# A four-layer graph network: the last layer run as one stage, block by block, with no barrier between its two sums

## The reference

```python
def _gcn_conv(x, W, b, src, dst, n):
    h = x @ W
    s = concat([src, loop]); d = concat([dst, loop])
    deg = segment_sum(ones_like(d), d, n)
    dinv = rsqrt(deg)
    msg = (dinv[s] * dinv[d])[:, None] * h[s]
    return segment_sum(msg, d, n) + b
h = relu(_gcn_conv(x, W1, b1, src, dst, n))
z = _gcn_conv(h, W2, b2, src, dst, n)
x = _layernorm(x + z)
```

## Time and profile before

| | us |
|---|---|
| median of three runs | 4654.02 |
| the profiled execution's own time | 4652.1 |
| its span, first to last instruction | 4650.3 |
| busy: PE, DVE, POOL, ACT | 2810.4, 3001.2, 2727.2, 934.8 |
| last layer: first matmul of the first sum to the end of the span | 342.9 |

### The profile page before, as it was taken

How to read it: one execution, slowest core, us unless ns; L and a number is a source line. 1 busy time by engine, 2 the same in 40 slices (tenths; PEclk the granted TensorE clock), 3 DMA queues, 4 the chain that set the end, 5 groups by cost and what they waited for, 6 DMA issues and landing times. The chain is left out here.

```text
span 4650.3 us, 56109 instructions
## 1 busy us (share of the span) xinstructions
PE 2810.4 (60%) x18074; PEld 2599.7 (56%) x18075; DVE 3001.2 (65%) x6284; ACT 934.8 (20%) x781; POOL 2727.2 (59%) x2656
## 2 busy tenths in 40 slices
PE   1356656656614555556566456666666667994955
PEld 0356656656613555555556356655665657983744
DVE  6355655655676666676665477777777778996144
ACT  0121221211201222222221121221221123441000
POOL 0577777777705777777773277777777723551000
PEclk9566656656656677776668767777777779996977
DMA  1444444444404455445443356556655625540532
GB/s 20 109 98 110 102 99 109 100 102 109 98 21 103 134 135 136 136 132 136 135 133 90 84 138 154 147 146 153 153 144 149 153 56 123 115 106 1 171 95 92
DMA packets 169458, 526.18 MB, mean 113 GB/s; under 512 B 60851, under 2 KB 87800, under 8 KB 156470
## 3 DMA queue, kind: packets, MB, share of 16 engines
q1 hardware_dynamic: 74032, 299.78, 26.1%
q0 software_dynamic: 95264, 224.28, 18.6%
HBM read 456.40 MB, written 67.48 MB: 113 GB/s over the span
## 5 line engine op out<-in xcount | busy, mean ns | idle before, releaser
L544 POOL DMA_INDIRECT e0G<-table,e0src x858 | 851.9, 993 | 439.1 <-issue 405.1
L544 POOL DMA_INDIRECT e21G<-table,e21src x858 | 856.1, 998 | 408.1 <-issue 257.6
L1364 POOL DMA_INDIRECT t1G<-table,t1idx x806 | 789.7, 980 | 375.5 <-issue 242.0
L1437 PE MATMUL t1psW<-t1CO,t1G 128*128 128x192 f32 x1612 | 435.9, 434 | 303.9 <-issue 285.6
L1437 PEld LDWEIGHTS t1psW<-t1CO,t1G 128*128 128x128 f32 x1612 | 370.4, 258 | 312.2 <-issue 292.2
L568 PE MATMUL e21psQ<-Q,e21OT 121*128 x1716 | 412.5, 410 | 129.6 <-DVE e21G L682 54.3
L568 PEld LDWEIGHTS e21psQ<-Q,e21OT 121*128 121x128 f32 x1716 | 399.8, 326 | 141.4 <-issue 81.6
L561 PE MATMUL e0psQ<-Q,e0OT 121*128 x1716 | 398.7, 371 | 94.3 <-ACT e0OT L599 58.2
L561 PEld LDWEIGHTS e0psQ<-Q,e0OT 121*128 121x128 f32 x1716 | 396.6, 325 | 99.8 <-issue 99.8
L2103 POOL TENSOR_TENSOR e22Z<-e22Z,e22C 121x847 f32<-121x847 f32 (+1 forms) x104 | 200.1, 1955 | 259.0 <-ACT e22Z L2095 259.0
L584 PE MATMUL e21psA<-e21G,e21O 128*121 128x145 f32 x1716 | 272.4, 330 | 106.1 <-DVE e21G L733 106.1
(11 more groups left out here) (428 smaller groups left out, 5250.8 us busy)
## 6 DMA issues: line engine op xcount, KB each, us to landing
e0dstb<-in_dst_p SPq DMA_DIRECT2D x27, 1996.5 KB
e21dstb<-in_dst_p SPq DMA_DIRECT2D x27, 1996.5 KB
e22C<-counts SPq DMA_DIRECT2D x26, 1487.0 KB
Q<-in_type_p SPq DMA_DIRECT2D x62, 416.0 KB
counts<-X SPq DMA_DIRECT2D x13, 1487.0 KB
planes<-SKIP SPq DMA_DIRECT2D x26, 743.5 KB
counts<-RES SPq DMA_DIRECT2D x13, 1487.0 KB
e31C<-planes SPq DMA_DIRECT2D x26, 743.5 KB
```

The lines of the kernel that those rows point to most:

```text
L544: nc.gpsimd.indirect_dma_start(out=G[:, u, t, 0:width], out_offset=None, in_=table, in_offset=bass.IndirectOffsetOnAxis(ap=src[:, u, t:t + ...
L1364: nc.gpsimd.indirect_dma_start(out=G[:, q % 2, t, :], out_offset=None, in_=table, in_offset=bass.IndirectOffsetOnAxis(ap=idx[:, q * GT + t ...
L1437: mmi = nc.tensor.matmul(psW[:, k % 2, 0:WIN * NBAS], G[:, q % 2, t, :], CO[:, k % 2, i].rearrange("p b w -> p (b w)"), start=(i == 0), st ...
```

## The change

The first projection stays. The other five stages become one function, `last_layer`, with one block of engine programs.

TensorE, in the first sum: after the 26 matmuls of block b it waits until its own last matmul is done, and only then gives the buffer back (`buffer_free`), turns the finished rows of block b-1 (`turn`) and multiplies those of block b-2 with W2 (`make`). In the second sum it waits in the same way after every block. VectorE, in the first sum: `take` adds the three parts and then into `SKIP` (so `RES` is not cleared and `SKIP` not added later), one operation scales and adds the bias, and `row` scales the product with W2 and splits four blocks at a time into a second set of parts, `HP2`. Relu is ScalarE's copy out of PSUM. In the second sum VectorE finishes each block as it comes and normalizes two blocks at a time; SyncE stores two blocks at a time. W2 and both biases are loaded ahead of the first counts. The counts of the second sum go through the same ring and are loaded as the first sum frees buffers. The only meeting point left is `parts_ready`: the second sum starts when all seven groups of `HP2` are written.

The diff, without the allocation of buffers:

```diff
@@ -171,10 +171,8 @@
 
         with ExitStack() as ctx:
             g["HP"] = ctx.enter_context(nc.sbuf_tensor("HP", [BN, NB, 3, D], BF16))
-            for c in (1, 2):
-                project(g, f"p3{c}", [(f"L3_gnn_W{c}", None)], tab[128], "gcn", source=X if c == 1 else RES)
-                dense_sum(g, f"e3{c}")
-                gcn_finish(g, f"f3{c}", f"L3_gnn_b{c}", out if c == 2 else None)
+            project(g, "p31", [("L3_gnn_W1", None)], tab[128], "gcn")
+            last_layer(g, out)
@@ -2155,6 +2153,228 @@
             dve.drain()
 
 
+def last_layer(g, out):
+    nc, a, X, RES, SKIP, HP, planes, eye, cnt1 = (g[k] for k in ("nc", "a", "X", "RES", "SKIP", "HP", "planes", "eye", "cnt1"))
+    RING = NB // 2
+    GRP = 4
+    NGRP = -(-NB // GRP)
+    STORES = (16 * 8, 16 * 6)
...
+        S = {n: sem(n) for n in ("consts", "waited", "buffer_free", "summed", "taken", "row_ready", "row_turned", "row_copied", "row_made",
+                                 "row_taken", "parts_ready", "summed2", "taken2", "var_ready", "rooted", "block_ready")}
...
+        @block.sync
+        def _(sp):
+            n = n_planes(sp)
+            def load(b, k, done):
+                sp.wait_ge(S["buffer_free"], done + 1)
+                sp.sem_inc(S["waited"], 1)
+                sp.dma_start(C[:, b % RING].rearrange("p h d -> p (h d)"),
+                             planes[bass.ds(k * NB + b, 1)].rearrange("a l n -> (a l) n")).then_inc(counts_in[b % RING], 16)
+            def store(k, i):
+                sp.wait_ge(S["block_ready"], k * (NB // 2) + (i + 1))
+                sp.sem_inc(S["waited"], 1)
+                if 2 * i + 2 < NB:
+                    sp.dma_start(out[2 * i * BN:(2 * i + 2) * BN].rearrange("(b p) f -> p b f", p=BN), z[:, i % 2]).then_inc(stored[i % 2], 16)
+                else:
+                    sp.dma_start(out[2 * i * BN:(2 * i + 1) * BN], z[:, i % 2, 0]).then_inc(stored[i % 2], 16)
+                    sp.dma_start(out[(2 * i + 1) * BN:N], z[0:N - (2 * i + 1) * BN, i % 2, 1]).then_inc(stored[i % 2], 16)
+            sp.dma_start(w2[:], a["L3_gnn_W2"]).then_inc(S["consts"], 16)
+            for i in range(2):
+                sp.dma_start(bias[:, i, :], a[f"L3_gnn_b{i + 1}"].partition_broadcast(BN)).then_inc(S["consts"], 16)
+            with sp.Fori(0, n) as k:
+                for b in range(NB):
+                    load(b, k, k * NB + b)
+            with sp.Fori(0, n) as k:
+                for b in range(NB):
+                    load(b, k, n * NB + k * NB + b)
+                    if b % 2 == 1 and b >= RING:
+                        store(k, b // 2 - RING // 2)
+                for i in range((NB - 1) // 2 - RING // 2 + 1, NB // 2):
+                    store(k, i)
+            for u in range(2):
+                sp.wait_ge(stored[u], n * STORES[u] + 16)
+                sp.sem_inc(S["waited"], 1)
+        @block.tensor
+        def _(pe):
+            n = n_planes(pe)
+            def sums(b, parts, made):
+                for h in range(NB):
+                    mmi = nc.tensor.matmul(ps[0:BN, b % 2, 0:3 * D], C[:, b % RING, h, :],
+                                           parts[:, h].rearrange("p k f -> p (k f)"), start=(h == 0), stop=(h == NB - 1))
+                mmi.then_inc(made, 1)
+            def turn(b, k):
+                pe.wait_ge(S["row_ready"], k * NB + (b + 1))
+                pe.wait_ge(S["row_copied"], k * NB + (b + 1))
+                nc.tensor.transpose(psT[:, b % 2, 0:BN], y[:, b % 2, :], eye[0:BN, 0:BN]).then_inc(S["row_turned"], 1)
+            def make(b, k):
+                pe.wait_ge(S["row_copied"], k * NB + (b + 3))
+                pe.wait_ge(S["row_taken"], k * NB + (b + 1))
+                nc.tensor.matmul(psY[0:BN, b % 2, 0:D], hT[:, b % 2, :], w2[:], start=True, stop=True).then_inc(S["row_made"], 1)
+            pe.sem_inc(S["buffer_free"], RING)
+            pe.sem_inc(S["row_made"], 2)
+            pe.wait_ge(S["consts"], 48)
+            with pe.Fori(0, n) as k:
+                for b in range(NB + 2):
+                    if b < NB:
+                        pe.wait_ge(counts_in[b % RING], k * 32 + (b // RING * 16 + 16))
+                        pe.wait_ge(S["taken"], k * NB + (b + 1))
+                        pe.sem_inc(S["waited"], 1)
+                        sums(b, HP, S["summed"])
+                        pe.wait_ge(S["summed"], k * NB + (b + 1))
+                        pe.sem_inc(S["buffer_free"], 1)
+                    if 1 <= b <= NB:
+                        turn(b - 1, k)
+                    if b >= 2:
+                        make(b - 2, k)
+            with pe.Fori(0, n) as k:
+                for b in range(NB):
+                    pe.wait_ge(counts_in[b % RING], n * 32 + k * 32 + (b // RING * 16 + 16))
+                    pe.wait_ge(S["taken2"], k * NB + (b + 1))
+                    if b == 0:
+                        pe.wait_ge(S["parts_ready"], n * NGRP)
+                    pe.sem_inc(S["waited"], 1)
+                    sums(b, HP2, S["summed2"])
+                    pe.wait_ge(S["summed2"], k * NB + (b + 1))
+                    pe.sem_inc(S["buffer_free"], 1)
+        @block.scalar
+        def _(act):
+            n = n_planes(act)
+            act.sem_inc(S["row_copied"], 2)
+            with act.Fori(0, n) as k:
+                for b in range(NB):
+                    act.wait_ge(S["row_turned"], k * NB + (b + 1))
+                    act.wait_ge(S["row_made"], k * NB + (b + 1))
+                    nc.scalar.activation(hT[:, b % 2, :], psT[:, b % 2, 0:BN], ACT.Relu).then_inc(S["row_copied"], 1)
+            with act.Fori(0, n) as k:
+                for i in range(NB // 2):
+                    act.wait_ge(S["var_ready"], k * (NB // 2) + (i + 1))
+                    nc.scalar.activation(var[:, i % 2, :], var[:, i % 2, :], ACT.Sqrt).then_inc(S["rooted"], 1)
+        @block.vector
+        def _(dve):
+            V = nc.vector
+            dr = dve.drain
+            n = n_planes(dve)
+            def take(b, made, count, taken, acc):
+                dve.wait_ge(made, count)
+                V.tensor_reduce(part[:, b % 2], ps[0:BN, b % 2, 0:3 * D].rearrange("p (k f) -> p f k", k=3), AX.X, ALU.add).then_inc(taken, 1)
+                dr()
+                V.tensor_tensor(acc, acc, part[:, b % 2], ALU.add)
+                dr()
+            def row(b, k):
+                dve.wait_ge(S["row_made"], k * NB + (b + 3))
+                V.tensor_scalar(RES[:, b, 0:D], psY[0:BN, b % 2, 0:D], cnt1[:, b:b + 1], None, ALU.mult).then_inc(S["row_taken"], 1)
+                if b % GRP == GRP - 1 or b == NB - 1:
+                    b0 = b - b % GRP
+                    m = b + 1 - b0
+                    full, hp, r = RES[:, b0:b + 1, 0:D], HP2[:, b0:b + 1], rest[:, 0:m, :]
+                    dr()
+                    V.tensor_copy(hp[:, :, 0, :], full)
+                    dr()
+                    V.tensor_tensor(r, full, hp[:, :, 0, :], ALU.subtract)
+                    dr()
+                    V.tensor_copy(hp[:, :, 1, :], r)
+                    dr()
+                    V.tensor_tensor(r, r, hp[:, :, 1, :], ALU.subtract)
+                    dr()
+                    V.tensor_copy(hp[:, :, 2, :], r).then_inc(S["parts_ready"], 1)
+            def norm_start(i, k):
+                u = i % 2
+                V.tensor_reduce(mean[:, u, :], z[:, u], AX.X, ALU.add)
+                dr()
+                V.tensor_scalar(mean[:, u, :], mean[:, u, :], 1.0 / D, None, ALU.mult)
+                dr()
+                V.tensor_tensor(z[:, u], z[:, u], mean[:, u, :].unsqueeze(2).broadcast_to([BN, 2, D]), ALU.subtract)
+                dr()
+                V.tensor_tensor(sq[:], z[:, u], z[:, u], ALU.mult)
+                dr()
+                V.tensor_reduce(var[:, u, :], sq[:], AX.X, ALU.add)
+                dr()
+                V.tensor_scalar(var[:, u, :], var[:, u, :], 1.0 / D, EPS, ALU.mult, ALU.add).then_inc(S["var_ready"], 1)
+            def norm_end(i, k):
+                u = i % 2
+                dve.wait_ge(S["rooted"], k * (NB // 2) + (i + 1))
+                V.reciprocal(var[:, u, :], var[:, u, :])
+                dr()
+                V.tensor_tensor(z[:, u], z[:, u], var[:, u, :].unsqueeze(2).broadcast_to([BN, 2, D]), ALU.mult).then_inc(S["block_ready"], 1)
+            for u in range(2):
+                dve.sem_inc(stored[u], 16)
+            dve.sem_inc(S["taken"], 2)
+            dve.sem_inc(S["row_taken"], 2)
+            dve.sem_inc(S["taken2"], 2)
+            dve.wait_ge(S["consts"], 48)
+            with dve.Fori(0, n) as k:
+                for b in range(NB + 2):
+                    if b < NB:
+                        take(b, S["summed"], k * NB + (b + 1), S["taken"], SKIP[:, b, :])
+                        if b >= 2:
+                            dve.wait_ge(S["row_turned"], k * NB + (b - 1))
```

(52 more changed lines are left out.)

## The result

Four runs of the changed kernel took 4585.46 to 4594.29 us, median 4587.41; four of the kernel before had a median of 4653.06. The ratio is 0.986, 95% interval 0.9843 to 0.9878: 65.6 us faster by the medians, where 75.5 were forecast (4578.5; range 4564 to 4606).

A forecast was written before the change was run, and what follows sets the result against it. The last layer was taken as a chain of differently bound stages; two sums stay, stretches without sums shrink. Terms summed to 267.4 against 342.9 us, 75.5 less: 4576.6, plus 1.9 for the median, 4578.5; range 4564 to 4606.

The forecast's parts named there:

- The stretch between the sums: From the first sum's last matmul until TensorE may start the second sum: 7.8 us instead of 65.2, set by VectorE's remaining work.
- The tail: From the last matmul to the end of the span: 9.5 us instead of 52.0, with VectorE's part near 5.0.
- VectorE beside the sums: VectorE's per-block work hides beside TensorE's: 4.9 us against a 4.85 block first, 6.8 per pair against 2 x 4.5 second.
- Turn and product: Extra TensorE work between blocks of the first sum: 0.33 us each time, 24 times, 7.9 us in all.
- The wait for itself: TensorE waiting for its own last matmul after each block: 0.30 us lost at each of 50 seams, 15.0 in all.
- Its bounds of 0.1 and 1.24: Limits on TensorE's self-wait loss per block: 0.1 us from a ScalarE release, 1.24 from the attention pass.
- the sign that was named for it: Reduction intervals above 5.2 us in the first sum and 4.8 in the second would mean self-wait or following waits underpriced.
- The three things named: At each block's seam: last matmul running out, semaphore coming back, first weights loading; together put at 0.30 us a block.
- The start: Three small loads ahead of the first counts delay TensorE by 1.5 us: 1.1 of issue, at most 1.7 of transfer.
- the two rivals of the clock: In both sums, broken matmul streams lower the clock: swinging, 4623 us at 0.83 (10%), or slower than before (3%).
- as dear as in the attention pass: Rival: TensorE's self-wait at block seams costs 1.24 us instead of 0.30, 47 us more, 4625; chance 6%.
- The counts of the second sum: Rival: counts not loaded when the second sum starts, so TensorE waits 6.9 us again, 4585; chance 4%.

## Why the prediction was right, and where it was off

Direction, range and mechanism held: the layer was a chain of stages, and the two stretches without sums fell from 72.26 and 51.94 to 13.75 and 8.43.

- **The stretch between the sums** held: 7.5 us from TensorE's last matmul of the first sum (4449.43) to the first of the second, forecast 7.8, and its order held too: row 23 and its split, rows 24 and 25, the split of two. The second sum started at a low clock as assumed, and lost a little less by it: 6.3 instead of 7.08 us to its first reduction.
- **The tail** held: 8.43 against 9.5. VectorE's part took 5.3 instead of 5.0, the landing of the stores and what follows it 2.4 instead of 3.8. Without the finishing beside the sums it is 40.0 longer, as the run with the second convolution finished last showed.
- **VectorE beside the sums** held: in the second sum every reduction found it waiting for TensorE, for 0.59 us at least, and the interval didn't change when its work was taken out.
- **Turn and product** held to the hundredth: 0.326 against 0.33.
- **The wait for itself** is the step that failed in size: 0.30 was put, 0.56 and 0.60 measured, 29.1 us instead of 15. Its bounds of 0.1 and 1.24 held it, and the sign that was named for it came: the second sum's interval of 4.83 lies above 4.8. The three things named (run-out, way back, bare load) cost 0.33, the release included, so that sum was good. Left out was that a drained queue (one with no matmul left to run) also lays bare what stands behind the wait: in the second sum two more waits and an increment, 0.25 us in most seams and 0.27 in the mean. The prediction had seen that two waits fit into the 0.065 of a seam and that the queue could hide them, and took them as free; they are free only behind a full queue. The Trainium skill (Advanced Engine Details and Errata, "Miscellaneous Facts") gives 50 to 100 ns for reading a semaphore. The 0.12 us for each of the two instructions in the drained seam is a little above that, and the nothing that they cost behind queued matmuls is below it.
- **The start** was put at 1.5 and came to 3.3, above its upper bound of 1.1 + 1.7; in the seven other runs with these loads in place it came to 3.4 to 4.8. Moving the loads took 3.0 of the 3.3 back.
- **The rivals.** The clock stayed at 1.00 in both sums but for their starts, so the two rivals of the clock are out. The Trainium skill (TensorE: Matmul & The Clock Gate, "A second HAM failure mode: psum-queue depth-cycling") has the clock swing when TensorE idles briefly between groups of matmuls as banks are cycled; with gaps of 0.30 to 0.57 us a block and two banks in turn it did not swing here. The self-wait was not as dear as in the attention pass. The counts of the second sum were there in time; without their lead it would have cost not the 6.9 us forecast but 8.2, and a stall of the stores, 7.7 more.

By size: start +1.8, first sum +6.3, second sum +7.5, between and tail -1.1 each; 13.4 of the 75.5 not gained by the traces.

## What to carry to other kernels

Where TensorE is what everything waits for, a wait for its own last matmul has a price. Count the run-out of that matmul and every instruction between the wait and the next matmul, and let the engine that needs the news (here SyncE) wait for the matmul's semaphore itself, or release one block later, as the next one's 26 matmuls hide it. When stages of whole-layer operations stand between dense sums, doing them block by block beside the sums gave back about 102 of their 124 us here, and cost 37 us in the sums by what the new seams asked of TensorE. Small loads go behind the first large ones that someone is waiting for.

## What the runs showed of the hardware

- A self-wait of TensorE between matmuls of 384 columns, with one increment behind it, costs 0.33 us, in the middle of a block and at its end alike. Two more control instructions behind it (two waits and an increment) cost 0.25, and behind a full queue nothing.
- Every fifth block of the second sum the seam is 0.08 to 0.17 us longer (0.48 or 0.57 instead of 0.40), at the same blocks in every run without a stall that leaves TensorE's second sum as it is. With the next block's waits put ahead no seam is longer: all intervals are 4.55 or 4.56. Why was not tried.
- Of the three casts from float32 to bfloat16 of 121 x 384 elements the first took 0.43 us, as long as 121 x 512 take, and the other two 0.55. The slow ones read one run of 384 elements and write three pieces of 128; the fast one reads and writes three pieces. Whether that is the reason was not tried.
- A store of 121 KB issued among loads of 743.5 KB gave its buffer back only 19.6 us after its issue, and with the stores on a queue of their own VectorE still waited up to 7.1 us for one.
